# Reordering the prologue of a two-layer GNN kernel: names before weights, clears paced by gathers

## The reference

```python
h = jnp.maximum(_layernorm(x, axis=-1), 0.0)
x = x + _L0_gnn_ref(h, W_l, W_r, edge_index)       # mean of h[src] over the edges of each dst, @ W_l.T, + h @ W_r.T
h = jnp.maximum(_layernorm(x, axis=-1), 0.0)
x = x + _L1_gnn_ref(h, edge_index, edge_attr, ...)  # segment_sum(edge_attr, src), concat, three linear
                                                    # layers with silu and batch norm over all nodes
```

## Time and profile before

| | us |
|---|---|
| median of three runs | 1426.01 |
| lowest and highest | 1422.40 and 1430.45 |
| span of the profiled execution, first to last instruction | 1425.6 |
| time of that execution outside its span | not listed |
| POOL busy, share of the span | 881.3 (62%) |
| DVE busy | 1066.8 (75%) |
| PE busy | 1038.0 (73%) |
| ACT busy | 860.6 (60%) |

### The profile page before, as it was taken

How to read it: one execution, slowest core, us unless ns; L and a number is a source line. 1 busy time by engine, 2 the same in 40 slices (tenths; PEclk the granted TensorE clock), 3 DMA queues, 4 the chain that set the end, 5 groups by cost and what they waited for, 6 DMA issues and landing times.

```text
span 1425.6 us, 22736 instructions
## 1 busy us (share of the span) xinstructions
PE 1038.0 (73%) x5520; PEld 744.8 (52%) x5520; DVE 1066.8 (75%) x4684; ACT 860.6 (60%) x1688; POOL 881.3 (62%) x625
## 2 busy tenths in 40 slices
PE   0027766776766666665988898887878889999875
PEld 0015545555555445453565565555545766447765
DVE  2119888888886667666999899898874888787756
ACT  0017767776766555552777777876775556669610
POOL 7757888888888888876777777776761000002433
PEclk9989999999999888988999999999998999999999
DMA  9967888877776666657898999988978995216999
GB/s 331 371 253 170 212 213 209 223 160 173 164 163 142 152 146 137 137 136 186 208 237 222 234 239 225 236 213 218 231 198 270 363 333 183 88 59 228 406 408 369
DMA packets 202877, 315.38 MB, mean 221 GB/s; under 512 B 20913, under 2 KB 72535, under 8 KB 202785
## 3 DMA queue, kind: packets, MB, share of 16 engines
q1 hardware_dynamic: 135000, 266.54, 54.9%
q0 software_dynamic: 62720, 38.57, 22.4%
q10 hardware_dynamic: 5064, 9.29, 1.9%
HBM read 163.49 MB, written 150.84 MB: 220 GB/s over the span
## 4 chain that ended last, share of the span: by engine, by line
POOL 37%; DMA 28%; issue 18%; PE 11%; SPq 3%; DVE 2%; ACT 1%; another core or an unknown queue 0%; POOLq 0%; DVEq 0%; ACTq 0%
POOL acc L899 21%; POOL acc L919 9%; DMA acc<-tabs,target_b 8%; DMA acc<-zT,target_b 7%; DMA zT<-x_dram 7%; POOL xin L877 6%; PE ps L1740 6%; DMA xin<-acc 2%; DMA acc<-zT,tabs 1%; PE ps L1704 1%; PE ps L1707 1%; SPq L618 1%; PE ps L1710 1%; DMA res<-acc 1%; DMA zT<-z_dram 1%
## 5 line engine op out<-in xcount | busy, mean ns | idle before, releaser
L1601 PE MATMUL ps<-zT 128*128 128x512 f32 (+5 forms) x784 | 262.4, 483 | 167.1 <-ACT zT L1038 121.6
L899 POOL DMA_INDIRECT acc<-zT,tabs x196 | 316.8, 1616 | 82.2 <-issue 62.1
L1601 PEld LDWEIGHTS ps<-zT 128*128 128x128 f32 (+1 forms) x784 | 158.7, 209 | 294.4 <-issue 198.3
L919 POOL DMA_INDIRECT acc<-zT,target_b x100 | 157.2, 1572 | 56.2 <-issue 24.8
L1354 DVE BATCH_NORM_STATS2 zT<-zT 128x6 f32<-128x128 f32 (+1 forms) x384 | 79.4, 277 | 146.9 <-DMA zT<-in_x_dram 134.2
L919 POOL DMA_INDIRECT acc<-tabs,target_b x96 | 151.0, 1573 | 54.3 <-issue 25.2
L877 POOL DMA_INDIRECT xin<-in_x_dram,tabs x140 | 141.7, 1012 | 42.6 <-issue 41.7
L1593 PE MATMUL ps<-ident,zT 128*128 128x128 f32 (+1 forms) x784 | 113.3, 292 | 43.4 <-ACT zT L990 39.3
L998 ACT ACTIVATE hT<-ps 128x1024 f32<-128x1024 f32 (+1 forms) x100 | 99.8, 1000 | 43.7 <-PE ps L1593 23.6
L1593 PEld LDWEIGHTS ps<-ident,zT 128*128 128x128 f32 (+1 forms) x784 | 94.1, 152 | 57.3 <-ACT zT L990 48.8
L1479 DVE BATCH_NORM_STATS2 bst<-zT (+1 forms) x168 | 107.3, 683 | 18.5 <-ACT zT L1141 17.4
(11 more groups left out here) (201 smaller groups left out, 2279.7 us busy)
## 6 DMA issues: line engine op xcount, KB each, us to landing
acc<-bst SPq DMA_DIRECT2D x12, 2112.0 KB
acc<-bst SPq DMA_DIRECT2D x48, 528.0 KB
zT<-in_x_dram SPq DMA_DIRECT2D x48, 512.0 KB
zT<-acc SPq DMA_DIRECT2D x48, 512.0 KB
zT<-x_dram SPq DMA_DIRECT2D x42, 512.0 KB, 10.0
out_dram<-zT SPq DMA_DIRECT2D x42, 512.0 KB, 10.6
zT<-row_dram SPq DMA_DIRECT2D x49, 256.0 KB
zT<-in_edge_attr_dram SPq DMA_DIRECT2D x48, 256.0 KB
```

Of the source, the lines that this page charges most:

```text
L899: pool.indirect_dma_start(acc1, bass.IndirectOffsetOnAxis(ap=target_a[:, k, j:j + 1], axis=0), v[:, j, :], None, compute_op=ALU.add).then_ ...
L919: pool.indirect_dma_start(acc2, bass.IndirectOffsetOnAxis(ap=target_b[:, k, j:j + 1], axis=0), vrow_b[k % RING][:, j, :], None, compute_op ...
L1601: ins = nc.tensor.matmul(psA[:, 0:j + 1, 0:p], t[0:p, j, :], same[0:p, par, at:at + j + 1, 0:p], start=(j == ROWS - 1), stop=(j == 0))
```

## The change

Three things are moved and one small thing is added. ACT issues the thirteen weight and vector loads after the staging copies of the names. SP no longer puts clears 2 to 5 between the writes of `row_dram` and of `half_dram`; after the two first `load_a` it issues clears 2 to 6, and in the sweep's step for round (0,1), behind `load_a(1,1)`, clears 7 to 11. Clear k from 3 on waits until `s_mem` has reached k; POOL increments that semaphore ten times, at every fifth gather of the store from the 18th gather of the kernel on (the second of round index 2).

```diff
+    PACED = 3
...
+    assert 5 * (ZPARTS - 1 - PACED) + 1 <= (PRE - 2) * ROWS
...
-        s_mem = sem("memsets_done")
+        s_mem = sem("memsets_done_then_gathers_begun_by_fives")
...
                 if ahead:
                     load_a(*ahead)
+                if type(now[0]) is int and now[:2] == (0, 1):
+                    clear_acc1(7, ZPARTS)
...
             def clear_acc1(lo, hi):
                 for k in range(lo, hi):
+                    if k >= PACED:
+                        sp.wait_ge(s_mem, 2 + k - PACED + 1)
                     sp.dma_start(acc1_z[k], zeros.unsqueeze(1).broadcast_to([P, 4 * ZREP, ZCOLS]))\
                         .then_inc(s_zero1, 16)
...
             sp.dma_start(row_dram[P:IC, :], row_stage[0:IC - P, 1, :]).then_inc(s_idx, 16)
-            clear_acc1(2, 6)
             sp.wait_ge(s_staged, 6)
...
             load_a(0, 1, False, False, 1)
-            clear_acc1(6, ZPARTS)
+            clear_acc1(2, 7)
             sweep(sp, step_a, (SPILLED, PRE), wide=True)
...
             def gather_pre(i):
 
                 for j in range(ROWS):
+                    if i > 1 and ((i - 2) * ROWS + j) % 5 == 1:
+                        pool.sem_inc(s_mem, 1)
...
             for t, v in ((icol[:, :].bitcast(i32), src_v), (raw, dst_v)):
                 act.dma_start(t[0:EDGE_TAIL, RF * ROWS:], v[1]).then_inc(s_idx, 16)
-            for t, w in ((wl, WlT), (wr, WrT), (w1a, W1[0:D, :]), (w1b, W1[D:2 * D, :]), (w2, W2), (w3, W3)):
-                act.dma_start(t[:, :], w).then_inc(s_w, 16)
-            for k, v in enumerate((b1, g1, be1, b2, g2, be2)):
-                act.dma_start(vecs[:, k:k + 1], column(v)).then_inc(s_w, 16)
-            act.dma_start(b3b[:, :], b3.partition_broadcast(P)).then_inc(s_w, 16)
             act.wait_ge(s_set, 1)
...
                 nc.scalar.activation(to[0:q, at, :], ps_k, ACT.Copy).then_inc(s_staged, 1)
+            for t, w in ((wl, WlT), (wr, WrT), (w1a, W1[0:D, :]), (w1b, W1[D:2 * D, :]), (w2, W2), (w3, W3)):
+                act.dma_start(t[:, :], w).then_inc(s_w, 16)
+            for k, v in enumerate((b1, g1, be1, b2, g2, be2)):
+                act.dma_start(vecs[:, k:k + 1], column(v)).then_inc(s_w, 16)
+            act.dma_start(b3b[:, :], b3.partition_broadcast(P)).then_inc(s_w, 16)
```

## The result

The changed kernel takes 1458.1 us (median of 4 runs, 1456.84 to 1459.99), the kernel before 1425.17 us in the same session (4 runs, 1422.4 to 1430.45): ratio 1.0213, 95% interval 1.0173 to 1.0253, 33 us slower. The forecast was 1413 us, in a range up to 1430. The profiled execution of after has a span of 1455.9 us and a time of its own of 1457.86 us, and every timed run of both kernels lists a span some 2 us under its time: my span was compared with the wrong thing, but the 0.4 us that I read as the time outside it hardly matters beside 33.

What follows compares the result with a forecast made beforehand. Phase A was taken as bound by POOL's queue, so an earlier first scatter moves everything. Waits of 13.46 us less 0.4 for increments give 13.1; 1425.6 - 13.1 = 1412.5, plus 0.4 outside the span: 1413 us, range 1409 to 1430.

Steps and rivals of the forecast that it cites:

- Names before weights: ACT's queue at the start: names staged by about 8.6 us, DVE starting at 22 us, 30 us earlier.
- Round (0,0) at the pace of (1,0): First round on DVE and ACT: 15.7 us from DVE's start at 22 us, product copied at 38 us.
- the sum with every pause kept: Round (0,0) taking 57.9 us as before: done at 80 us, before POOL asks at 97.3 us.
- Pauses stay, shifted: Rival: pauses not from clears; comparison of (0,1) at 81 us, POOL scatters near 109, about 1425 us; chance 0.12.
- The slower rival: Rival: clears 7 to 11 wait on SP behind (0,1)'s comparison; at 95 us first scatter at 123, 1439 us; chance 0.13.
- The prize of 13.1 us: POOL's waits before the first two scatters: 12.57 + 0.89 = 13.46 us saved, less 0.4 for increments.
- The copies of three rounds lying ready: After the first scatter: POOL's own issue is what is late next, as three rounds' copies already wait.
- Ten increments on POOL: Semaphore increments among POOL's early gathers: cost 0.4 us, bounds 0.4 and 3.0 us.
- phase A's length: POOL's phase A behind the first scatter: length unchanged.
- Pauses only in the profile: Rival: pauses exist only in the profiled execution, so the change has nothing to give, 1426 us; chance 0.27.

Runs made afterwards that it cites:

- the run in which POOL was held: Changed kernel with clears 2 to 11 ahead of the sweep, unpaced; POOL stops its early gathers until round (0,1) is copied: 1494.58 us, one run.
- names-only run: Kernel before with only ACT staging the names ahead of the weight loads, SP's order and clears as they were: 1427.91 us, ratio 1.0005.
- the clears ahead: Changed kernel with all ten paced clears (2 to 11) issued ahead of the sweep, none behind load_a(1,1): 1431.1 us, ratio 1.0042.
- the last timed version: Changed kernel, second clears one load earlier, unpaced; ScalarE's first two copies ahead of the square root; all 56 early store gathers spaced by small POOL clears: 1424.66 us, ratio 0.9966.

## Why the prediction was wrong

**Names before weights: right.** ScalarE stages the names from 8.00 to 9.09 us (8.6 forecast), and VectorE starts at 24.87 us (22).

**Round (0,0) at the pace of (1,0): the step that failed.** I put the copy at 38 us and the comparison of (0,1) at 44; they came at 97.18 and 104.83 us. Compared with the run in which POOL was held, 15.9 us from statistic to copy, the pace was right for a quiet POOL. I had the 59 us of the kernel before in hand and still priced the round undisturbed, on the argument that fewer clears would be queued. That laid the pauses at the clears' door with no row for it: the window from 100 to 105 us already showed a pause with idle DMA engines. The runs put in its place: POOL's train of indirect DMAs makes the pauses, and they last until about 1.40 us for each of them have passed. For round (0,0) I did check the sum with every pause kept (80 us); for the comparison of (0,1), on which SP's queue hangs, I did not carry it through, only as a rival with 0.12.

**"Pauses stay, shifted": right in kind, short in size.** It moved 59 us along with the start, to 81 us. The pauses don't move with the round; where POOL stops behind its 72 or 74 gathers they end at 105 to 108 us, whatever the start. The names-only run shows it barest: 2.9 us earlier at the start, 0.66 at the scatter.

**The slower rival: it happened.** Its place (SP's wait in `load_a(1,1)`) holds. Priced at 95 us it gave 1439; at 104.83 its own rule says 104.83 + 28 = 132.8 us for the first scatter, and 142.90 was measured. The term mis-sized there is the clears' 27.5 us: the rate of 5.6 us each is right, but from SP's issue to POOL's go it is 34.7, and two gathers of the loop (2.5 us) stand ahead of the scatter. From the end of the comparison to the scatter it is 38.1 us, so by an estimate from this the gain was gone at 109.88 - 38.1 = 72 us, not at 80.

**The prize of 13.1 us: wrong even where the comparison doesn't matter.** With the clears ahead the first scatter comes at 99.57, near the 97.7 forecast, and the kernel is 0.4% slower than before. I took the second scatter's wait for a fixed 1.19 us; it grew to 15.09, for the copy of (0,1). "The copies of three rounds lying ready" was wrong. Only in the last timed version, where both copies come before POOL asks, does POOL go straight through, and then the spacing itself takes 8 us of the prize.

**Ten increments on POOL, phase A's length: right.** The 72nd gather ends at 94.72 us with the increments among the gathers and at 94.48 without, 0.24 us later (0.4 forecast); phase A differs by 1.1 us of 546.

**"Pauses only in the profile": fell** as a forecast: the timed runs lose 33 us by the medians.

**A misreading on which nothing hangs.** It is not round (1,1) that needs all gathers of the store, as the text ahead and the prediction have it. By line 512 of the kernel (0,1) and (1,1) wait for the first two parts and the rounds from (2,1) on for the rest.

## What to carry to other kernels

When a transfer is put on a queue behind a wait, price that wait by the latest time at which it has been seen to end, not by the work ahead of it at its best; one misjudged wait cost 33 us for five clears that could have gone one load earlier. A pause whose inputs are ready has to be tied to a cause by a row before an edit counts on its going, and holding one suspect at a time (here clears, pacing, POOL) did it in three runs. An account that names a rate should then be held against every run by its count, also where the edit seemed to cure the pauses. After removing a wait on the engine that bounds the kernel, check the next wait on the same engine too: here the time went with the second scatter.

## What was unexpected of the hardware

A train of indirect DMAs on POOL at one in 1.26 us holds VectorE and ScalarE in pauses of 5 to 13 us, with a beat of mostly 1.40 us between. At one in 1.40 us the first two comparisons run nearly free of it, but waits of over 20 us with ready inputs come later. It makes no difference whether a gather has 128 or 64 rows, and full clears at 389 GB/s beside them do no harm. In the window from 65 us TensorE is busy for 0.00 us and its granted clock is 0.50, the 1.2 GHz level; from 110 us, with 3.66 us of work in 5, it is 0.82 on the mean.
